# Mixed expert tiles scattered in two passes, and full tiles read from their expert's weights in place

## What is computed

```python
x = x + jnp.tanh(g_xattn[0]) * _L0_xattn_ref(ctx_512, _layernorm(x, axis=-1), Wq, Wk, gamma_raw)
x = x + jnp.tanh(g_ffn[0]) * _L0_ffn_ref(_layernorm(x, axis=-1), ...)
...
def _L0_ffn_ref(hidden_states, ...):
    x = hidden_states.reshape(-1, Dd)
    shared = silu(x @ shared_gate_w) * (x @ shared_up_w) @ shared_down_w
    logits = x @ router_w
    top_val, top_idx = jax.lax.top_k(logits, K)                      # K = 2 of E = 8
    probs = zeros_like(logits).at[arange(T)[:, None], top_idx].set(sigmoid(top_val))
    xin = probs.T[:, :, None] * x[None]
    gate, up = split(einsum('etd,edf->etf', xin, gate_up_w))         # D = 512, I = 256
    expert_out = einsum('eti,eid->etd', silu(gate) * up, down_w)
    return shared + expert_out.sum(axis=0)
```

## Time and profile before

| | |
|---|---|
| median of 3 runs | 395.9 us (395.59 to 397.62) |
| the profiled execution | 397.1 us, of which the profile's span is 395.4 |
| TensorE busy | 367.4 us, 93% |
| VectorE, ScalarE, GpSimd busy | 256.2, 212.1, 142.1 us |
| chain that ended last | TensorE 71%, ScalarE 8%, DMA 7%, VectorE 7% |
| mean granted TensorE clock | 0.978 of full |

### The profile page before, as it was taken

How to read it: one execution, slowest core, us unless ns; L and a number is a source line. 1 busy time by engine, 2 the same in 40 slices (tenths; PEclk the granted TensorE clock), 3 DMA queues, 4 the chain that set the end, 5 groups by cost and what they waited for, 6 DMA issues and landing times.

```text
span 395.4 us, 7266 instructions
## 1 busy us (share of the span) xinstructions
PE 367.4 (93%) x2372; PEld 233.0 (59%) x2374; DVE 256.2 (65%) x858; ACT 212.1 (54%) x406; POOL 142.1 (36%) x114
## 2 busy tenths in 40 slices
PE   8957889989999999999999999999999999999970
PEld 4313478557845588457875475757545644567750
DVE  1799999999999689960846793645547654623310
ACT  3595788476653686435220575554556565652320
POOL 2200220030533342222215265463656655644422
PEclk9986999999999999999999999999999999999996
DMA  7999971166657633449241755544535353644244
GB/s 218 383 388 382 389 242 37 27 195 182 189 108 170 200 64 34 72 112 206 35 53 35 128 79 90 103 77 85 87 78 91 72 86 76 107 61 87 44 55 53
DMA packets 29357, 51.18 MB, mean 129 GB/s; under 512 B 4614, under 2 KB 7942, under 8 KB 29318
## 3 DMA queue, kind: packets, MB, share of 16 engines
q0 software_dynamic: 9920, 22.16, 34.1%
q1 hardware_dynamic: 19110, 28.40, 20.8%
q10 hardware_dynamic: 288, 0.13, 0.1%
HBM read 28.60 MB, written 22.09 MB: 128 GB/s over the span
## 4 chain that ended last, share of the span: by engine, by line
PE 71%; ACT 8%; DMA 7%; DVE 7%; issue 3%; POOL 1%; SPq 1%; POOLq 1%; DVEq 0%; ACTq 0%
PE gate_up L1317 25%; PE down L1367 15%; PE gate_up L1326 8%; PE gate_up L1332 6%; PE down L1358 4%; PE turned_x L1295 4%; DMA out_dram<-y_sb,idx 3%; ACT junk L713 3%; PE front L1274 2%; DMA xs<-in_x_dram 2%; DMA out_dram<-y_sb,tmp 1%; DMA out_dram<-tmp,idx 1%; PE front L1182 1%; ACT x L750 1%; ACT sim L708 1%
## 5 line engine op out<-in xcount | busy, mean ns | idle before, releaser
L1317 PEld LDWEIGHTS gate_up<-xT,w_shgu 128*128 128x128 f32 x1024 | 117.6, 192 | 11.7 <-issue 10.4
L1317 PE MATMUL gate_up<-xT,w_shgu 128*128 128x128 f32 x1024 | 121.0, 276 | 1.5 <-ACT xT L761 1.1
L565 POOL DMA_INDIRECT xg<-x_rows,idx x34 | 52.2, 1534 | 43.5 <-DMA x_rows<-payl 13.5
L589 POOL DMA_INDIRECT out_dram<-y_sb,idx x20 | 35.9, 1793 | 54.0 <-DMA out_dram<-y_sb,idx 20.9
L815 ACT ACTIVATE y_sb<-down,gates 128x512 f32<-128x512 f32 x42 | 28.8, 687 | 36.5 <-PE down L1367 24.9
L1367 PE MATMUL down<-w_dn,hT 128*128 x100 | 47.0, 596 | 0.0
L2045 DVE COPY sim<-w_gu 128x2048 f32 x36 | 42.1, 1221 | 1.9 <-issue 1.0
L713 ACT ACTIVATE junk<-sim,probe 128x512 int8<-128x512 f32 x44 | 31.2, 712 | 16.8 <-DVE probe L1730 9.9
L2053 DVE COPY w_shgu<-w_gu 128x2048 f32 x16 | 20.0, 1249 | 26.6 <-PE gate_up L1317 17.7
L826 ACT COPY xs<-w_dn 128x1024 f32 x36 | 36.0, 1045 | 2.0 <-issue 1.7
L2074 DVE SCALAR_TENSOR_TENSOR h<-gate_up,p_t,silu 128x256 f32<-128x256 f32 x18 | 8.7, 482 | 42.9 <-ACT silu L784 33.9
(11 more groups left out here) (241 smaller groups left out, 535.0 us busy)
## 6 DMA issues: line engine op xcount, KB each, us to landing
w_gu<-in_L_ffn_gate_up_w_dram SPq DMA_DIRECT2D x8, 1024.0 KB
xs<-in_x_dram SPq DMA_DIRECT2D x4, 1024.0 KB, 7.7
w_dn<-in_L_ffn_down_w_dram SPq DMA_DIRECT2D x8, 512.0 KB
out_dram<-xs SPq DMA_DIRECT2D x4, 1024.0 KB, 6.0
x_rows<-x SPq DMA_DIRECT2D x4, 1024.0 KB, 4.7
out_dram<-y_sb POOLq DMA_DIRECT2D x16, 256.0 KB
w_gu<-in_ctx_dram SPq DMA_DIRECT2D x4, 256.0 KB, 5.8
xg<-x_rows,idx POOLq DMA_INDIRECT x34
```

Source lines behind the costliest of these rows:

```text
L565: G.indirect_dma_start(out=xg[:, t % XG, :], out_offset=None, in_=x2_rows[0:2 * N, :] if t < EARLY else x2_rows[:, :], in_offset=bass.Indi ...
L589: G.indirect_dma_start(out=out[0:2 * N, :] if t < EARLY else out[:, :], out_offset=bass.IndirectOffsetOnAxis(ap=rows, axis=0), in_=y_at(j) ...
L1317: mm = TE.matmul(g_b[j % 2][:, f * P:(f + 1) * P], w_shgu[:, c, f * P:(f + 1) * P], xT[:, x_slot(j), c], start=(c == 0), stop=(c == DC - 1))
```

## The change

- `MIXED` is (9, 11, 13, 15, 18, 21, 24, 27, 30) in place of (9, 12, 15, 18, 20, 22, 24, 26, 28). The number of mixed tiles stays nine.
- `STAGED` is tile 33 alone. The other 15 full tiles are read from `w_gu` in place, with `turn_h` and `turned_h`, and without `stage_full` and the scaling of their rows.
- No fold: `fold`, `folded_y` and the nine matrices go. In their place `scatter_doubles(t)` scatters each mixed tile a second time, behind the scatter of the next tile. Its indices `idx_d` name the output row for a token's second rows, and spare rows for all others.
- New waits: a mixed tile's scatter waits for the second scatter of the mixed tile before, tile 32's scatter for all nine, and `y_of`, where it takes the buffer of a mixed tile, for that tile's second scatter too.
- The unit copies of `stage_up` stand four in a row everywhere.

```diff
-    MIXED = (9, 12, 15, 18, 20, 22, 24, 26, 28)
+    MIXED = (9, 11, 13, 15, 18, 21, 24, 27, 30)
...
-    STAGED = [t for t in range(EARLY + 1, MT) if t not in MIXED]
+    STAGED = [33]
...
+        idx_d = tmp[:, 3, 48:48 + MIX].bitcast(I32)
...
             def scatter(t):
...
                 if t == PAIR:
                     rows = idx_p
+                    pool.wait_ge(doubles_out, 16 * MIX)
                     pool.wait_ge(scatter_ready, 1)
                 if m is not None:
-                    pool.wait_ge(folded, m + 1)
+                    if m:
+                        pool.wait_ge(doubles_out, 16 * m)
                     pool.wait_ge(scatter_ready, 1)
...
+            def scatter_doubles(t):
+                m = MIXED.index(t)
+                pool.wait_ge(scattered, 16 * CHAIN.index(t) + 16)
+                G.indirect_dma_start(out=out[:, :], out_offset=bass.IndirectOffsetOnAxis(ap=idx_d[:, m:m + 1], axis=0),
+                                     in_=y_at(job_of("M", t)), in_offset=None, compute_op=ALU.add
+                                     ).then_inc(doubles_out, 16)
...
             scatter(19)
+            scatter_doubles(18)
             gather(24)
...
             scatter(31)
+            scatter_doubles(30)
             scatter(32)
             scatter(33)
...
             def y_of(j):
...
                     act.wait_ge(scattered, 16 * CHAIN.index(JOBS[k][1]) + 16)
+                    if mixed_at(k) is not None:
+                        act.wait_ge(doubles_out, 16 * mixed_at(k) + 16)
...
-            def folded_y(j):
-                act.wait_ge(fold_ps, mixed_at(j) + 1)
-                A.copy(y_at(j), f_b[0][:, :]).then_inc(folded, 1)
...
-            def fold(j):
-                m = mixed_at(j)
-                pe.wait_ge(y_done, j + 1)
-                pe.wait_ge(twins_done, 3)
-                if m:
-                    pe.wait_ge(folded, m)
-                TE.matmul(f_b[0][:, :], fold_m[:, m * P:(m + 1) * P], y_at(j), start=True,
-                          stop=True).then_inc(fold_ps, 1)
...
             down(34)
-            up(36, 34)
+            turn_h(35)
+            up(36)
             turn_rows(21)
             down(35)
             turn_h(36)
...
-                    V.tensor_scalar(fold_m[:, m * P:(m + 1) * P], others, row_f[:, m:m + 1], None, ALU.is_equal)
...
+                V.tensor_scalar(idx_d, unused[:, 0:MIX], dump, None, ALU.add)
...
             gate(27)
-            stage_full(13)
+            stage_up(2, 0)
+            stage_up(2, 1)
+            stage_up(2, 2)
+            stage_up(2, 3)
             weight_of(13)
```

More of the change, by code:

```diff
@@ L374, in flamingo_gated_block @@
         rows_weighed = sem("rows_weighed")
-        folded = sem("folded")
+        doubles_out = sem("doubles_out")
         gu_ps = sem("gu_ps")
@@ L1026, in _ @@
             turned_h(28)
+            stage_down(2, 0)
+            stage_down(2, 1)
             silu_of(29)
@@ L1029, in _ @@
             y_of(28)
-            stage_down(2, 0)
-            stage_down(2, 1)
-            folded_y(28)
+            turned_h(29)
+            stage_down(2, 2)
+            stage_down(2, 3)
             silu_of(30)
@@ L1035, in _ @@
             y_of(29)
-            stage_down(2, 2)
-            stage_down(2, 3)
+            turned_h(30)
+            stage_down(3, 0)
+            stage_down(3, 1)
             silu_of(31)
@@ L1041, in _ @@
             turned_h(31)
+            stage_down(3, 2)
+            stage_down(3, 3)
             silu_of(32)
@@ L1044, in _ @@
             y_of(31)
-            stage_down(3, 0)
-            stage_down(3, 1)
-            folded_y(31)
+            turned_h(32)
+            stage_down(4, 0)
+            stage_down(4, 1)
             silu_of(33)
@@ L1050, in _ @@
             y_of(32)
-            stage_down(3, 2)
-            stage_down(3, 3)
+            turned_h(33)
+            stage_down(4, 2)
+            stage_down(4, 3)
             silu_of(34)
@@ L1059, in _ @@
             y_of(34)
-            stage_down(4, 0)
-            stage_down(4, 1)
-            folded_y(34)
+            turned_h(35)
+            stage_down(5, 0)
+            stage_down(5, 1)
             silu_of(36)
@@ L1066, in _ @@
             turned_h(36)
-            stage_down(4, 2)
-            stage_down(4, 3)
+            stage_down(5, 2)
+            stage_down(5, 3)
             silu_of(37)
@@ L1083, in _ @@
             y_of(38)
-            stage_down(6, 0)
-            stage_down(6, 1)
-            folded_y(38)
+            turned_h(39)
+            stage_down(6, 2)
+            stage_down(6, 3)
             silu_of(40)
@@ L1119, in _ @@
             y_of(44)
-            folded_y(44)
+            turned_h(45)
+            stage_down(8, 2)
+            stage_down(8, 3)
             silu_of(46)
@@ L1313, in up @@
                     for f in range(F2 // P):
-                        if f == F2 // P // 2 and folds is not None:
-                            fold(folds)
                         for c in range(DC):
@@ L1321, in up @@
                     for c in range(DC):
-                        if c == DC // 2 and folds is not None:
-                            fold(folds)
                         for r in range(4):
@@ L1594, in _ @@
             down(25)
-            up(27, 25)
+            turn_h(26)
+            up(27)
             turn_rows(12)
             down(26)
+            turn_h(27)
             up(28)
@@ L1604, in _ @@
             down(28)
-            up(30, 28)
+            turn_h(29)
+            up(30)
             turn_rows(15)
             down(29)
+            turn_h(30)
             up(31)
@@ L1614, in _ @@
             down(31)
-            up(33, 31)
+            turn_h(32)
+            up(33)
             turn_rows(18)
             down(32)
+            turn_h(33)
             up(34)
@@ L1631, in _ @@
             down(36)
-            up(38, 36)
+            turn_h(37)
+            up(38)
             turn_rows(23)
@@ L1638, in _ @@
             down(38)
-            up(40, 38)
+            turn_h(39)
+            up(40)
             turn_rows(25)
@@ L1645, in _ @@
             down(40)
-            up(42, 40)
+            turn_h(41)
+            up(42)
             turn_rows(27)
@@ L1652, in _ @@
             down(42)
-            up(44, 42)
+            turn_h(43)
+            up(44)
             turn_rows(29)
@@ L1659, in _ @@
             down(44)
-            up(46, 44)
+            turn_h(45)
+            up(46)
             turn_rows(31)
             down(45)
+            turn_h(46)
             up(47)
@@ L2013, in find_twins @@
                 if k == 2:
-                    both = fold_m[:, MIX * P:(MIX + 1) * P]
+                    both = join_m
                     link(V.tensor_scalar(both, f_b[0][:, P:2 * P], row_p[:, 0:1], None, ALU.is_equal))
@@ L2289, in _ @@
             weight_of(14)
-            stage_up(2, 0)
-            stage_up(2, 1)
-            stage_full(14)
             gate(29)
+            stage_up(3, 0)
+            stage_up(3, 1)
+            stage_up(3, 2)
+            stage_up(3, 3)
             weight_of(15)
-            stage_up(2, 2)
-            stage_up(2, 3)
             gate(30)
-            stage_full(16)
             weight_of(16)
             gate(31)
[L2301 to L2313, removed]
             stage_up(4, 0)
@@ L2317, in _ @@
             stage_up(4, 3)
[L2318 to L2322, removed]
+            weight_of(17)
+            gate(32)
+            weight_of(18)
+            gate(33)
+            weight_of(19)
+            gate(34)
             stage_up(5, 0)
@@ L2326, in _ @@
             stage_up(5, 3)
+            weight_of(20)
+            gate(35)
+            weight_of(21)
+            gate(36)
+            weight_of(22)
             gate(37)
[L2328 to L2331, removed]
             stage_up(6, 0)
@@ L2335, in _ @@
             stage_up(6, 3)
+            weight_of(23)
+            gate(38)
+            weight_of(24)
             gate(39)
-            stage_full(25)
             weight_of(25)
             gate(40)
-            weight_of(26)
             stage_up(7, 0)
@@ L2349, in _ @@
             weight_of(28)
+            gate(43)
             stage_up(8, 0)
```

64 lines of the change are left out of this document (32 added, 32 removed).

## The result

The changed kernel takes 399.8 us in the median of 6 runs (398.95 to 402.93), the kernel before 395.9 (395.46 to 398.05). The ratio is 1.0101, with a 95% interval of 1.0063 to 1.0138: some 4 us slower. The forecast was 398.5 in a range of 391.5 to 403, slower with a chance of 0.5.

A forecast was written before the change was run, and what follows sets the result against it. Bound by TensorE and, nearly level, the scatter chain. Chain: 239.0 + 23 x 5.6 + 7.6 + 0.8 = 376.2, plus 10.6 and 0.5 is 387.3; 10.7 more gives span 398.0, forecast 398.5 us, range 391.5 to 403.

The forecast's parts named there:

- the likeliest case: Scatter chain sets the end at 387: copies cost it 9.5 to 14 us, time 397.5 to 402; chance 0.35.
- The chain of scatters has little to spare: GpSimd, scatters 9 to 32: 6.33 us a step against 5.6 at least, 0.7 spare, 17 us in all.
- The waits for a second scatter, 4 x 1.9: Scatters of tiles 11, 13, 15, 32 wait for a second scatter: step 7.5 us, +1.9 each, +7.6 in all.
- The new wait of `y_of` on tile 11: ScalarE waits 4 us for tile 9's second scatter: 0.8 us on the chain, 3 us on TensorE.
- The copies against the scatters, 10.6 us: VectorE's unit copies stretch GpSimd's scatters: +8.2 behind tiles 15, 18, 21, 24, +2.4 in the first part.
- The sum: Scatter 32 at 387.3, 10.7 us to the end, span 398.0; adjusted to the median, 398.5 us.
- 0.5 for data ahead in the queue: Data of a gather and a second scatter ahead of scatter 32 in its queue: 0.5 us on the chain.
- TensorE's folds, -9.5: TensorE in mixed tiles: a fold costs 1.06 us, and nine go, so -9.5 us.
- Reading in place, +0.24 a tile: TensorE, 15 full tiles: wide up products -0.13, turns of h +0.22, turning rows +0.15; +3.6 us in all.
- VectorE and ScalarE at nothing: Their changed work hides under TensorE's and costs nothing; job 26's late gate, seen once, costs about half a microsecond of TensorE.
- The rival that TensorE sets the end: Change pays: collisions under 6 us, TensorE ends near 379 to 381, time 391.5 to 394; chance 0.25.
- the pattern it read from the rows: Scatter starting under a VectorE copy waits for its end, works 1.46 us; meeting another, ends 0.08 behind that copy.

The follow-up runs named there:

- short copies: Changed kernel with the 36 unit copies on VectorE cut from 2048 to 64 columns (wrong weights in mixed tiles): 391.66 us, ratio 0.9864.
- both repairs: Changed kernel with 128 more spare rows for the second scatters and y buffers in the order 0, 2, 1: 389.97 us, ratio 0.9834.
- the order experiment: Changed kernel with y buffers in the order 0, 2, 1 from job 26, so tile 11 no longer writes tile 9's buffer: 399.18 us, ratio 1.0059.
- the pair with short copies: Unit copies cut to 64 columns in the changed kernel (391.66 us, ratio 0.9864) and in the kernel before (396.84 us, ratio 0.9998).
- the bound: Changed kernel with own spare rows for second scatters, y buffers in the order 0, 2, 1 and unit copies cut to 64 columns: 387.19 us, ratio 0.9747.

## Why the prediction was right

The time (398.5 for 399.8), the direction and the mechanism of the likeliest case held; that the time came so close is in part luck, for the sizes of the terms missed both ways. By the steps:

- **The chain of scatters has little to spare, a step is 5.6 us.** Right; without second scatters three late steps are 5.9, 5.6 and 5.5 (365.36 - 359.50, and on to 376.50).
- **The waits for a second scatter, 4 x 1.9: too low.** Four steps of 8.1 us in the mean for 7.5, with short copies too (32.2 us together). That is 9.8 us above 5.6 each, for 7.6. A second scatter lands 5.0 to 5.4 us after its issue and not 4.9. With both repairs the four steps are back at 22.9 us, 9.4 less.
- **The new wait of `y_of` on tile 11.** Right in place: it ended at 253.7 where I had 251.5, and scatter 9 and 10 were themselves 1 to 2 us late. From the end of tile 11's down product, 247.1, ScalarE waited 6.6 us for my 4, and TensorE stood idle for 3.15 us for my 3. That it would also halve the clock for some 4 us I did not see; it cost 2.0 us more. All of it together was worth 1.7 us in the order experiment, with intervals that overlap, for the chain sets the end. Six later calls of `y_of` waited for second scatters too, with ScalarE idle for 22.8 us in all ahead of them; TensorE shows no wait above 0.65 us behind them.
- **The copies against the scatters, 10.6 us: too high, right in kind.** Shown by the pair with short copies: some 9 us of time in one kernel, none in the other. I had the gate of tile 21 near 305 and scatter 19 near 305.6; they came at 305.51 and 306.94. But in the chain from scatter 9 to 32 the copies cost 7.1 us. The steps behind tiles 15, 18, 21 and 24 are 1.39, 1.15, 1.98 and 0.94 above 5.6, where I had 2.05 each.
- **The sum.** Above 5.6 a step the chain has 9.8 us of waits, 7.1 of copies, and 3.0 that stay with short copies and that no run takes apart: 19.9. I had 7.6, 10.6 and 1.3 (0.8 for the early stall, 0.5 for data ahead in the queue): 19.5. The errors of +2.2, -3.5 and +1.7 nearly cancel. No run shows the 0.5 by itself.
- **TensorE's folds, -9.5.** The kernel with folds and reading in place ends TensorE at 384.3. Without folds it ends at 375.2 (with short copies and both repairs) or at 373.6 (without second scatters): 9.1 to 10.7 us.
- **Reading in place, +0.24 a tile: mis-sized.** TensorE ends at 384.3 for 383.3 with all folds kept, so +0.07 a tile. I took the 0.59 for turning rows as standing behind wide products; in the earlier trace rows it stands behind a mixed tile's. Behind the wide products of a full tile it is 0.44, as behind narrow ones. The term of 3.6 us should have been 1. It did no harm because TensorE did not set the end.
- **VectorE and ScalarE at nothing.** Right but for job 26, where the gate was late: `down` ended at 234.75 and the turn of h came at 234.90, 0.15 for my half microsecond.
- **The rival that TensorE sets the end** is what the bound makes of the change: with own spare rows, the buffer order and short copies TensorE does set the end. Its end at 375.2, and the prediction's 12.1 us to the end of the span and 0.5 to the median, give 387.8 for 387.2 measured.

On the rule of the Trainium skill, page "SBUF — State Buffer", section "SBUF: two separate sides": the runs agree that VectorE's copies hold up GpSimd's issue of a DMA, some 9 us of it here. They don't agree that the first holds the ports for its whole instruction. At 306.94 the scatter begins under a copy, and two further copies run wholly within its 2.65 us. In the earlier trace rows already the copy at 367.63 starts 0.74 us into the scatter of 366.89 and takes 1.37 us for 1.23, and it is the scatter, which began first, that is stretched. So the prediction was wrong that its sum is the one by the rule; it is the one by the pattern it read from the rows.

## What to carry over

When work leaves the busiest engine, first look for the chain that ends beside it, and count how much a step of that chain has to spare; here it was 0.7 us, and of nine scatters set beside it four came with a wait that cost 2.5 us each. A copy that costs nothing beside one order of DMA issues costs microseconds beside another, so compare the same copies at two places before calling them free. When a wait guards something that nobody reads (the spare rows), give each writer its own.

## What the runs showed that I had not expected

- After 3.15 us without a product TensorE's granted clock was 0.51 and 0.64 in two stretches of 2 us (256 to 260), and 1.00 from 260 on; while it was idle, and in the stretch where work began again at 254.84, the profile still showed 1.00. From one down product to the next it cost 2.0 us.
- A second scatter, most of whose rows go to spare rows, is no cheaper than a first: 5.0 to 5.4 us from issue to landing, against 4.9 in the earlier trace rows.
- Turning 128 rows of 512 takes 0.44 us behind products on whole 128-row weights, narrow or wide, and 0.59 behind those on 32 rows; a turn of h takes 0.22 and 0.37 in the same way.
